# Graph, attention and expert layer on one core: order and form of the key/value sums and of the payload

## The reference

```
xn = layernorm(x)
x  = x + gnn(xn, edges) + mix(xn)
x  = x + moe(layernorm(x))                     # 8 experts, top 1, capacity 489

gnn:  h = A xn      (A: sum of weight * xn[src] per dst)
      two more A products with a linear layer and a softmax each, then tanh(mean)
mix:  q, k, v = xn wq.T, xn wk.T, xn wv.T      # 4 heads of 64
      k = layernorm over a head(k) * g_k + b_k ; v = layernorm over a head(v) * g_v + b_v
      kv = sum over all 3125 rows of k^T v / 3125   (per head, 64x64)
      mix = (q kv) wo.T + bo
```

## Time and profile before

| | |
|---|---|
| median of 3 runs | 1262.71 us |
| profiled execution | 1251.25 us, its span 1249.5 us |
| granted TensorE clock, mean | 0.971 |
| TensorE busy | 1135.6 us, 91% |
| VectorE busy | 722.6 us, 58% |
| ScalarE busy | 307.3 us, 25% |
| GpSimd busy | 131.7 us, 11% |

### The profile page before, as it was taken

One profiled execution on the slowest core, in us unless ns is written; L12 is line 12 of the kernel. 1 busy time (PEld: TensorE's weight loads), 2 busy tenths in 40 slices (PEclk: granted clock), 3 DMA queues, 4 the chain that ended last, 5 costly groups with the idle time before them and its releaser, 6 DMA issues.

```text
span 1249.5 us, 14411 instructions
## 1 busy us (share of the span) xinstructions
PE 1135.6 (91%) x5049; PEld 728.1 (58%) x5049; DVE 722.6 (58%) x1713; ACT 307.3 (25%) x1009; POOL 131.7 (11%) x175
## 2 busy tenths in 40 slices
PE   1579889889999999999998999999999669999995
PEld 1246556567666666666667444454557636666664
DVE  5889889888777777777774010112346704444433
ACT  1445445442121221222221011110111122222220
POOL 1111112110000000000000000000222621111111
PEclk9989889999999999999999899999999879999998
DMA  6101011012233333333223898878796663333420
GB/s 167 11 6 42 1 43 43 1 44 84 85 118 119 118 126 131 137 127 155 85 85 152 319 365 296 294 288 301 262 307 212 209 204 107 112 119 112 150 70 7
DMA packets 65814, 175.41 MB, mean 140 GB/s; under 512 B 16559, under 2 KB 49098, under 8 KB 53710
## 3 DMA queue, kind: packets, MB, share of 16 engines
q1 hardware_dynamic: 50824, 120.70, 28.2%
q10 hardware_dynamic: 10598, 45.72, 9.4%
q0 software_dynamic: 4320, 8.04, 1.8%
HBM read 113.82 MB, written 63.01 MB: 142 GB/s over the span
## 4 chain that ended last, share of the span: by engine, by line
PE 83%; DVE 7%; ACT 5%; issue 2%; DMA 2%; SPq 0%; POOLq 0%; POOL 0%; DVEq 0%; ACTq 0%
PE ps L1509 21%; PE ps L1369 20%; PE ps L1352 11%; PE ps L1615 9%; PE ps L1604 9%; PE ps L1327 3%; ACT W L644 2%; PE ps L1273 2%; PE ps L1394 2%; ACT RING L656 1%; PE ps L1371 1%; DVE W L898 1%; ACT RING L641 1%; PE ps L1545 1%; PE ps L1313 1%
## 5 line engine op out<-in xcount | busy, mean ns | idle before, releaser
L1509 PE MATMUL ps<-RING,RY 128*128 128x512 f32 (+2 forms) x750 | 277.0, 526 | 6.3 <-issue 6.3
L1369 PE MATMUL ps<-RING,XX 128*128 128x512 f32 x600 | 282.6, 593 | 0.2
L1509 PEld LDWEIGHTS ps<-RING,RY 128*128 128x128 f32 x750 | 134.0, 192 | 132.4 <-issue 130.2
L1352 PEld LDWEIGHTS ps<-RING 128*128 128x128 f32 x1250 | 162.9, 193 | 53.4 <-issue 50.4
L1352 PE MATMUL ps<-RING 128*128 128x128 f32 x1250 | 170.3, 277 | 9.5 <-ACT RING L656 9.5
L666 ACT COPY RING<-ps 128x512 f32<-128x512 f32 (+1 forms) x157 | 91.6, 583 | 335.3 <-PE ps L1352 318.7
L937 DVE TENSOR_TENSOR RING<-iota_n,RY 128x512 f32<-128x512 f32 (+1 forms) x157 | 107.9, 687 | 69.7 <-PE ps L1352 63.4
L1369 PEld LDWEIGHTS ps<-RING,XX 128*128 128x128 f32 x600 | 102.8, 191 | 72.5 <-issue 72.4
L943 DVE TENSOR_TENSOR RING<-iota_n,RY 128x512 f32<-128x512 f32 (+1 forms) x157 | 107.0, 681 | 0.0
L576 POOL DMA_INDIRECT xbuf_dram<-XX,sidx x25 | 25.2, 1010 | 631.9 <-DVE sidx L1196 626.1
L946 DVE TENSOR_TENSOR RING<-RING,RY 128x512 f32<-128x512 f32 x132 | 90.0, 682 | 0.0
(11 more groups left out here) (243 smaller groups left out, 1299.6 us busy)
## 6 DMA issues: line engine op xcount, KB each, us to landing
RING<-adj_dram SPq DMA_DIRECT2D x62, 1280.0 KB, 6.4
adj_dram<-RING ACTq DMA_DIRECT2D x31, 1280.0 KB, 4.5
XT<-in_L_ffn_w SPq DMA_DIRECT2D x8, 1024.0 KB, 8.1
RING<-in_L_ffn_w SPq DMA_DIRECT2D x8, 1024.0 KB, 6.8
rbuf_dram<-W SPq DMA_DIRECT2D x8, 516.0 KB, 5.6
RING<-rbuf_dram SPq DMA_DIRECT2D x8, 516.0 KB, 3.7
xbuf_dram<-W SPq DMA_DIRECT2D x8, 512.0 KB, 3.2
RING<-xbuf_dram SPq DMA_DIRECT2D x8, 512.0 KB, 4.8
```

Source lines behind the costliest of these rows:

```text
L1352: last = nc.tensor.matmul(o[:, i * P:(i + 1) * P], h[:, 0, i, :], h[:, 1, i, :], start=True, stop=(j != s))
L1369: last = nc.tensor.matmul(ps[:, ACC + dd, :], w, at, start=(j == 0), stop=True, skip_group_check=True)
L1509: last = nc.tensor.matmul(o, (Y if l == 0 else S0)[:, j, :], RING[:, slot_of[g % 5], i * across + first:i * across + first + w], start=(j ...
```

## The change

- ScalarE: at a turn the root of `hvar` is taken before the squares of the tile, no longer behind them. VectorE: the variance is computed at the head of the iteration, before `prepare` and `spread`.
- TensorE: `kvprod` moves from behind `product` to behind `turn`, before apply.
- Key sums: `khat` gets a 129th column of ones behind each value block of 128, so that key half times value block gives the product and the key sum in 129 columns. The one-column products go.
- Value sums: GpSimd adds the value half of each khat into `vacc` (128x256 float32); one product with ones in iteration 30 sums it over the partitions into bank PROD.
- Payload: `pay` and `V` change their order from field, pair to pair, field, and the five multiplications become one with 2340 elements.
- All builds alternate between banks 0 and 1.

```diff
@@ GpSimd
-            for it in range(NT + 1):
-                if it:
+            for it in range(NT + KV_LAG + 1):
+                if 1 <= it <= NT:
...
+                if it > KV_LAG:
+                    m = it - KV_LAG - 1
+                    gp.wait_ge(s_khat, m + 1)
+                    ge(gp, s_vsum, m)
+                    gp.tensor_tensor(vacc..., vacc..., khat[m % 2][:, 2:4, 0:P], ALU.add).then_inc(s_vsum, 1)
@@ ScalarE
-                    squares(it)
                 if it in range(KT, NT + 1, KT):
                     g = it // KT - 1
                     act.wait_ge(s_hvar, g + 1)
                     nc.scalar.activation(hrs[:, g % 2, :], hvar[:, g % 2, :], ACT.Sqrt).then_inc(s_hroot, 1)
+                if it < NT:
+                    squares(it)
@@ VectorE, constants
+            for i in range(2):
+                v.memset(khat[i][:, 2:4, P:P + 1], 1.0)
+            v.memset(vacc, 0.0)
@@ VectorE, prepare (the same operations on a strided view)
+                field = lambda f: pay[:, t0 * C2:t1 * C2, f, :]
+                pairs = lambda x: x.rearrange("p (c i) -> p c i", i=2)
...
@@ VectorE, slot
-                for f in range(5):
-                    last = v.tensor_tensor(V[:, b, f * SW:(f + 1) * SW]..., ohp[b]..., pay[:, f, j * WC:(j + 1) * WC]..., ALU.mult)
-                last.then_inc(s_pay, 1)
+                v.tensor_tensor(V[:, b, :].rearrange("p (c f s i) -> p c f s i", f=5, s=NR, i=2),
+                                ohp[b].rearrange("p (c s i) -> p c s i", s=NR, i=2).unsqueeze(2).to_broadcast([P, C2, 5, NR, 2]),
+                                pay[:, j * C2:(j + 1) * C2, :, :].unsqueeze(3).to_broadcast([P, C2, 5, NR, 2]),
+                                ALU.mult).then_inc(s_pay, 1)
@@ VectorE, normed
                 ge(dve, s_kvt, m - 1)
+                ge(dve, s_vsum, m - 1)
@@ VectorE, kv_tail
                 dve.wait_ge(s_kvt, NT)
+                dve.wait_ge(s_vtot, 1)
@@ VectorE, loop
+                turn = it in range(KT, NT + 1, KT)
+                if turn:
+                    head_var(it // KT - 1)
                 if 1 <= it < NT:
                     if it in starts:
                         prepare(starts.index(it))
                     spread(it)
-                turn = it in range(KT, NT + 1, KT)
-                if turn:
-                    head_var(it // KT - 1)
@@ TensorE, kvprod
-                nc.tensor.matmul(ps[:, 1, 0:D], ones_f[:, :], k[:, D:2 * D], start=first, stop=True, skip_group_check=True)
                 for c in range(2):
-                    kh = k[:, c * P:(c + 1) * P]
-                    nc.tensor.matmul(ps[:, 1, D + c:D + c + 1], kh, ones_f[:, 0:1], start=False, stop=True, skip_group_check=True)
-                    last = nc.tensor.matmul(ps[:, KVACC, c * P:(c + 1) * P], kh, k[:, D + c * P:D + (c + 1) * P], ...)
+                    last = nc.tensor.matmul(ps[:, KVACC, c * (P + 1):(c + 1) * (P + 1)], k[:, c, 0:P], k[:, 2 + c, :], ...)
@@ TensorE, build
-                if u <= SINGLE:
-                    ge(pe, s_bev, u)
-                elif u == SINGLE + 1:
-                    pe.wait_ge(s_kvp, 1)
-                else:
-                    pe.wait_ge(s_bev, u - 1)
+                ge(pe, s_bev, u - 1)
@@ TensorE, loop
                 if it < NT:
                     product(it)
-                if KV_LAG <= it < NT + KV_LAG:
-                    kvprod(it - KV_LAG)
...
                 if it + 1 < NT:
                     turn(it + 1)
+                if KV_LAG <= it < NT + KV_LAG:
+                    kvprod(it - KV_LAG)
+                if it == NT + KV_LAG:
+                    pe.wait_ge(s_vsum, NT)
+                    pe.wait_ge(s_sq, NT)
+                    nc.tensor.matmul(ps[:, PROD, 0:D], ones_f[:, :], vacc, start=True, stop=True).then_inc(s_vtot, 1)
```

More of the change, by code:

```diff
@@ L98 @@
 T1_AT, M_AT = 34, 36
-SINGLE = 36
-def bank_of(u):
-    return 0 if u <= SINGLE else u % 2
 def ge(eng, semaphore, value):
@@ L167, in graph_program @@
         V = W[:, 0:2340].bitcast(BF16).rearrange("p (b n) -> p b n", b=2)
-        khat = [W[:, 2340 + 512 * i:2852 + 512 * i] for i in range(2)]
-        sq = W[:, 3364:3876]
+        khat = [W[:, 2340 + 516 * i:2856 + 516 * i].rearrange("p (g n) -> p g n", n=P + 1) for i in range(2)]
+        sq = W[:, 3372:3884]
         dflat = W[0:EP, 0:425].bitcast(I32)
@@ L343, in graph_program @@
         s_kvt = sem("s_kvt")
+        s_vsum = sem("s_vsum")
+        s_vtot = sem("s_vtot")
         s_kacc = sem("s_kacc")
@@ L556, in _ @@
                     gp.tensor_tensor(X1[:, it, :], X1[:, it, :], bo_b[:, :], ALU.add).then_inc(s_bo, 1)
+                if it > KV_LAG:
+                    m = it - KV_LAG - 1
+                    gp.wait_ge(s_khat, m + 1)
+                    ge(gp, s_vsum, m)
+                    gp.tensor_tensor(vacc.rearrange("p (c n) -> p c n", c=2), vacc.rearrange("p (c n) -> p c n", c=2), khat[m % 2][:, 2:4, 0:P], ALU.add).then_inc(s_vsum, 1)
             gp.wait_ge(s_m, 1)
@@ L665, in evac @@
                 act.wait_ge(s_bmm, u + 1)
-                nc.scalar.copy(RING[:, n % 2, u % 5 * 512:u % 5 * 512 + w], ps[:, bank_of(u), 0:w]).then_inc(s_bev, 1)
+                nc.scalar.copy(RING[:, n % 2, u % 5 * 512:u % 5 * 512 + w], ps[:, u % 2, 0:w]).then_inc(s_bev, 1)
                 if u == last_unit(n):
@@ L1312, in slots @@
                 for c in range(WC):
-                    last = nc.tensor.matmul(ps[:, MISC, 0:5 * NR], k[:, c // 2, :, c % 2], p[:, :, c // 2, :, c % 2], start=(c == 0), stop=(c == WC - 1))
+                    last = nc.tensor.matmul(ps[:, MISC, 0:5 * NR], k[:, c // 2, :, c % 2], p[:, c // 2, :, :, c % 2], start=(c == 0), stop=(c == WC - 1))
                 last.then_inc(s_slotted, 1)
@@ L1331, in kvprod @@
                 pe.wait_ge(s_khat, m + 1)
-                first = m == 0
                 k = khat[m % 2]
-                nc.tensor.matmul(ps[:, 1, 0:D], ones_f[:, :], k[:, D:2 * D], start=first, stop=True, skip_group_check=True)
                 for c in range(2):
-                    kh = k[:, c * P:(c + 1) * P]
-                    nc.tensor.matmul(ps[:, 1, D + c:D + c + 1], kh, ones_f[:, 0:1], start=False, stop=True, skip_group_check=True)
-                    last = nc.tensor.matmul(ps[:, KVACC, c * P:(c + 1) * P], kh, k[:, D + c * P:D + (c + 1) * P], start=first and c == 0, stop=True, skip_group_check=True)
+                    last = nc.tensor.matmul(ps[:, KVACC, c * (P + 1):(c + 1) * (P + 1)], k[:, c, 0:P], k[:, 2 + c, :], start=(m == 0 and c == 0), stop=True, skip_group_check=True)
                 last.then_inc(s_kvt, 1)
             def build(u):
-                o = ps[:, bank_of(u), :]
+                o = ps[:, u % 2, :]
                 h = hot[u % 4]
-                if u <= SINGLE:
-                    ge(pe, s_bev, u)
-                elif u == SINGLE + 1:
-                    pe.wait_ge(s_kvp, 1)
-                else:
-                    pe.wait_ge(s_bev, u - 1)
+                ge(pe, s_bev, u - 1)
                 pe.wait_ge(s_wgt if u < LEAD else s_hot, u + 1)
```

36 lines of the change are left out of this document (17 added, 19 removed).

## The result

The changed kernel takes 1268.95 us (median; the kernel before beside it 1260.8): ratio 1.0067, interval 1.0049 to 1.0084. It is slower by 8.4 us; the prediction was 1245, 17.5 faster. Of its eight runs one took 6021.6 us and is not in the ratio. A second time the ratio was 1.0046 (1.0029 to 1.0062), with the kernel before at 1251.2 us: both kernels were some 10 us shorter there.

The account below looks back on a forecast made before the run. It took TensorE's 8.35 us loop (ScalarE's copy and squares, build, turn, apply) and turn stalls as the bound; 7.0 + 8.6 - 0.9 + 2.8 = 17.5 us (1.40%) gained gave 1245 us, range 1236 to 1257.

Parts of the forecast that it names:

- Part 2: TensorE's key product behind turn: costs 0.47 us, loop 8.82, wait before build 0.5 to 1.8, stall of 4.74 gone.
- three groups: Product 7 to 22, five iterations each: 45.3 us against 48.2, 2.9 gained each, 8.6 in all.
- Rivals, A: TensorE's clock falls in ordinary iterations, 3 us a fall; in every second, 10 us slower, 1273; chance 0.10.
- turn delays: TensorE late where head roots are made, every fifth iteration: first 2.6 us, then 1.2 each, bounds 0 and 3.
- end stretch: Product 24 to the build of iteration 33, set by VectorE: 39.8 us against 42.6, 2.8 gained.
- Up to product 7: Start of the kernel: clock fall after second payload goes, first turn 2.6 late; 7.0 us gained, 6.3 if fall stays.
- Root first: ScalarE's root before squares, VectorE's variance first: stall of 4.26 us before scaling goes, 3 to 4 before variance.
- Payload: VectorE's five multiplications as one: 1.38 us at unchanged pace, 0.27 us saved per iteration.
- rival B: VectorE's single payload multiplication runs at half pace: 1257 us; chance 0.08.
- Part 5: Two banks for all TensorE builds: no idle ends with the single bank, so nothing gained.
- Part 3: Value sums on GpSimd: khat waits for the sum of two tiles before, taken as long done.
- loss per add: Time each GpSimd value-sum add costs VectorE: 0.65 us taken, bounds 0 and 0.8.

Follow-up runs that it names:

- second profile: The changed kernel itself, unaltered, run again: ratio 1.0046 to the kernel before.
- idle filled: Changed kernel plus six small float32 products on TensorE between slots and build, their output overwritten: 1242.8 us, ratio 0.9931 to the kernel before.
- the shadow version: Changed kernel with the key product moved from behind turn to between slots and build: 1236.9 us, ratio 0.9892 to the kernel before.

## Why the prediction was wrong

**The step that failed: Part 2's "the wait before the build grows from 0.5 to 1.8", priced at nothing.** The sum has the three groups at "5 x 8.82 + 1.2 = 45.3", with no falls in ordinary iterations; they took 50.7 each. Their price stood under "Rivals, A" only. The prediction had the mechanism there, with "1.8 us of idle where it had 0.5", and gave it 0.10 because at the earlier trace rows one build after 1.81 us had kept its clock. That row was true and proved nothing: three of the 17 builds behind 1.89 us keep it as well. A's price was too high (3 us a fall, taken from one behind a stall of 4.74; measured 1.67), its count too low ("in every second"; measured fourteen of 19). That its 10 us slower is near the measured 8.4 is therefore luck. 14 x 1.67 = 23 us; the falls hid the turn delays that were predicted (2.6 and three of 1.2), so the stretch from product 5 to 24 misses its forecast by 17.3. Of the 26 us between forecast and result, 6.9 more are the end stretch, and 1.8 the start.

Point by point:
- **Up to product 7: held in the first profile, not in the second.** Product 7 comes 5.95 us earlier (1.9 in the second profile), 7.0 were predicted. The fall after the second payload did not go (product 3 took 3.44 us, behind an idle of 1.84), so product 5 gained only 1.1, not 2.9; "if the fall stays, 6.3" was the nearer figure.
- **Loop and idle of Part 2: held**, 8.80 and 1.89 against 8.82 and 1.8. The khat stall of 4.74 is gone. But in all, the part costs 20 us where it stands alone, with the old key product (1.0167), and 21 in the changed kernel, against the place in the shadow.
- **Root first: held.** No stall before the scaling; 10.3 us by itself. The wait before the variance was 5.09, in the place of 3 to 4, and hidden in the long iterations. The delay of 1.2 per turn is 1.6 to 3.6 where the ordinary iterations have no falls (idle filled; the 3.6 has one fall in it).
- **Payload: held**, 1.36 to 1.42 us against 1.38 in twenty of 25, 1.85 in the other five, and no half pace (rival B fell).
- **Part 5 (two banks) and the 129th column:** no run has either of them alone. Builds in one bank again, with value sums on TensorE, left the groups as they were (167.8 and 167.3).
- **"Long done" (Part 3): failed.** khat waits for GpSimd ten times, 1.8 us at most. The sum two tiles back is late because GpSimd takes it in its fixed order behind records and bias add of its iteration, and these wait for ScalarE. GpSimd's timeline:

```profile
111.82 0.38 POOL L548 TENSOR_TENSOR RY<-RY 128x26 f32<-128x26 f32 x1 [6.84 <-ACT RY L653]
...
112.47 0.73 POOL L554 TENSOR_TENSOR XX<-XX,bo_b 128x256 f32<-128x256 f32 x1
113.16 0.69 POOL L559 TENSOR_TENSOR RY<-RY,W 128x256 f32<-128x256 f32 x1
```

VectorE's:

```profile
113.94 0.69 DVE L929 TENSOR_TENSOR W<-RING,hrs 128x512 f32<-128x512 f32 x1 [1.84 <-POOL RY L559]
```

The khat of tile 4 starts at 113.94, when the sum of tile 2, which starts at 113.16, is done. In the groups this costs nothing that the runs can tell (167.3 and 167.8). The loss per add was near what was taken (0.49 measured on a hot, 0.65 taken).

- **End stretch: failed**, 6.9 us off. Scaling was done 10.05 us after product 24, as worked out (4.2 + 4.2 + 1.6), but the second strip-out came at 29.6, not 26.8: one wait of 0.83 and five hots stretched by 0.49. Behind it TensorE worked at half clock (0.52 from 296.70 to 303.85), so VectorE's tail began 7.15 us after the strip-out began where 3.2 were counted. The prediction had priced these products at full clock, and they stand behind an idle of 4.62 us. In the second profile the stretch is 45.2 us, 5.4 over the forecast.

By the rows of before alone, rival A deserved far more than 0.10: of the three idles near 2 us, two had brought falls, and the changed kernel was to meet such an idle in every iteration.

## What to carry to other kernels

A product that moves out of another engine's shadow costs twice: its own time in the loop, and the idle that it leaves, which can cost more through the clock (0.45 us and 1.2 us per iteration here). One row that kept its clock at such an idle is no bound; ask how often the kernel would meet it. If a late operand is the reason for the move, look for a later place inside the shadow (slots, key product, build: 21 us better), and remember that what a slow loop hides, such as late turns or a helper engine's queue, comes back when the loop gets short.

## What was not expected of the hardware

- The idle alone doesn't decide a fall. From product 5 to 24 of the changed kernel, 17 builds came behind 1.88 to 1.90 us of idle, and three of them brought no fall; the two behind 1.47 and 1.04 brought none either, nor did 1.40 in the ordinary iterations of the shadow version. The place of the fall drifts. TensorE's builds in iterations 7 to 10 of the changed kernel:

```profile
101.25 1.23 PE L1353 MATMUL ps<-RING 128*128 128x128 f32 x8 [1.90 <-ACT RING L659]
111.72 1.44 PE L1353 MATMUL ps<-RING 128*128 128x128 f32 x8 [1.90 <-ACT RING L659]
122.19 1.65 PE L1353 MATMUL ps<-RING 128*128 128x128 f32 x8 [1.89 <-ACT RING L659]
132.65 1.84 PE L1353 MATMUL ps<-RING 128*128 128x128 f32 x8 [1.90 <-ACT RING L659]
```

  The clock falls 0.2 us earlier in the build each time (1.23 to 1.84 us for what takes 1.13), until in the next one, at 143.10, it doesn't fall; then the falls come behind the build, and the same again from 183.37 (1.41) to 214.75 (2.02), and none at 225.20. So one row of such an idle tells only where it stood in this drift. The Trainium skill (TensorE: Matmul & The Clock Gate, "What's actually happening") says that the chip judges activity in a window that runs free of the kernel; the drift agrees with it, and no run here shows the window itself.
- An add of 128x256 float32 on GpSimd beside VectorE operations of 128x512 float32 costs both engines: 1.17 instead of 0.68 us, and 1.07 instead of 0.64 to 0.69. The rows of the end stretch show how. The add is issued at 284.31, while the hot of 284.16 runs, and gets some 0.4 us longer; the next hot begins 0.45 us after the add did. That next hot, of 284.76, gets 0.49 us longer; the add ends 0.62 us after its start, at 285.38. So each is held up for about the rest of the other. The Trainium skill (SBUF — State Buffer, "Who interferes with whom") says that a VectorE operation with two inputs in SBUF contends with a GpSimd operation that reads it, and that the pair of ports which they share is an exclusive lock; these rows agree with it.
